# A second bias's column sums in split operands, moved behind a factor product, and one product's banks taken in another order

## The chip, the cores and the metric

The kernel runs on one core of one Trainium2 chip. The metric is the device time of one execution, in microseconds, the median over several runs. TensorE (PE in the views, PEld for its weight loads), VectorE (DVE), ScalarE (ACT), GpSimd (POOL) and SyncE (SP, here a queue that issues transfers) each run their own list of instructions in order and wait for one another through semaphores.

## The reference, cut to what matters

```python
def _L0_cond_ref(x, adapter_mapping, W, b, lora_As, lora_Bs):      # B, T = 8, 256; 1024 in, 1024 out; rank 16
    base_out = jnp.einsum('bti,oi->bto', x, W) + b
    lora_h = jnp.einsum('bti,bir->btr', x, lora_As[adapter_mapping])
    return base_out + jnp.einsum('btr,bro->bto', lora_h, lora_Bs[adapter_mapping]) * 2.0

def _L1_cond_ref(x, adapter_ids, base_weight, base_bias, lora_A_w, lora_B_w):
    result = jnp.einsum('bsd,od->bso', x, base_weight) + base_bias
    h = jnp.einsum('bsd,brd->bsr', x, lora_A_w[adapter_ids])
    return result + jnp.einsum('bsr,bor->bso', h, lora_B_w[adapter_ids])

x = x + _L0_cond_ref(x, itok_B_0_23, W0, b0, A0, B0)
x = x + _L1_cond_ref(x, itok_B_6_15, W1, b1, A1, B1)
```

With U = I + W0 (transposed) and V = I + W1 (transposed) the two layers are one map: x U V, plus a low-rank part for each batch, plus a bias row c = b0 V + b1. The edits concern c.

## The kernel before, in words

**Fused weight (span 0 to about 113 us).** U V, 1024 by 1024, is built from quadrants of 512 by 512 with seven products, M1 to M7, instead of eight. Each operand is split in two float32r numbers, a high part (`high`, a cast on ScalarE) and a low part (`low`, a subtraction on VectorE), and each product of 128x128 weights with a 128x512 operand is three matmuls: high by high, high by low, low by high (L1036, L1040, L1041). A product has four row blocks of twelve matmuls (`row_block`), one to a PSUM bank. `a_banks` are banks 0 to 3, `b_banks` banks 4 to 7.

**Order on TensorE around the change.** M6 adds onto `a_banks`. Then come two matmuls of `ones_b` (128x128 ones in float32) with `bias_sum` (128x1024 float32, the partial products of c, one row to a partition), L1160: they sum over the partitions, into `b_banks[1]` and `b_banks[2]`, and count `c_summed`. Then the factor product `gt_passes` (24 matmuls, L1054 to L1056) goes into `b_banks[0]` and counts `gt_summed`. Then M5, whose row block into a `b_bank` adds onto a copy of M6's `a_bank` that ScalarE puts there (`put_e`, counted by `e_put`), then M4 onto `a_banks`, with a transposition (L1062) after its second block.

**Order on ScalarE there.** `put_e(3)`, the high part of `d11`, the high rows of c (`c_hl[0]`, L551, two copies from the banks), `put_e(1)` and `put_e(2)` (each behind VectorE's low rows of c), `gt_copy(1)` (L429), `put_e(0)`, the high part of `t3`, then the first batch's operands (`high_x`, L462) mixed with the high parts of `d22` (L566) and, later, `d21` (L570).

**Order on VectorE there.** The low parts of b1's rows (L928), `t2` = `d11` + `t3` (L649), the low rows of c (L938), the low part of `d11` (L646), sums of the first batch (L727, L734), the low part of `t3` (L646), the batch's low parts (L720) mixed with those of `d22` (L706, L707), the low part of `t2`, small fills (L964, L968) that end in `pad_set`, then `d21` and `t4` (L713, L715) mixed with `g_copy(1)` (L670) and `factors` (L755 to L759). Place 4 of `ops` holds `us3`, then `us2`, which M6 reads, then `t3`.

**SyncE's queue there.** The rows of b1 (L314) and of c (L322) are written to DRAM, come back as the stacked operand `rb` (L276), and the next batch's x is loaded (L268).

**Batches (from about 113 us).** For each of eight batches TensorE runs `p1` to `p7`, seven products of the fused weight with combinations of x, twelve matmuls each (L1188 to L1190), one product of x with the low-rank factors (`h_product`, L1214), and four matmuls of the stack (`ranks`, L1195). In the first batch the order is p1, p6, h, p7, p2, p5, p4, `fill_z`, p3. Before p1 it waits for `pad_set`; p7 waits for VectorE's `make_u2` (L793), and `fill_z` for `make_u4` (L800). Between these two VectorE runs, in order, the low part of `t1`, `stack_h`, the low part of `t4`, `make_u3` (L806), the second batch's low parts and sums, and the low part of its S2 (L720), whose cast on ScalarE (L462) waits for the sum L734.

Of the kernel before, what the change touches and what calls it, by code (L numbers as in the profile page):

```python
# [5 lines left out]
F32 = mybir.dt.float32  # L6
F32R = mybir.dt.float32r
# [30 lines left out]
def lora_pair(nc, xT, W0, W1T, A0, B0T, A1T, B1, b0, b1, idx0, idx1, out):  # L38
# [15 lines left out]

    ORDER_M7 = (1, 2, 3, 0)
    ORDER_M6 = (2, 3, 0, 1)
    ORDER_LAST = (3, 1, 2, 0)

    with ExitStack() as ctx:
        def sb(name, shape, dt):  # L60
            return ctx.enter_context(nc.sbuf_tensor(name, shape, dt))

        def sem(name):
            return ctx.enter_context(nc.semaphore(name))

        idx = sb("idx", [1, 2 * B], I32)
        ones_b = sb("ones_b", [P, P], F32)
        b0_raw = sb("b0_raw", [P, KT], F32)
        b0_sum = sb("b0_sum", [P, KH], F32)
        ops = sb("ops", [P, 6, 2, QUAD], F32R)  # L70
# [42 lines left out]


        gt_raw = g_all[:, KH:KT, :].rearrange("p k n -> p (k n)")

        def raw(name):
            at = UNIT[name]
# [11 lines left out]
        def d22(part, k):  # L130
            return late[:, 4 + part, k * HALF:(k + 1) * HALF]
# [85 lines left out]
        bias_step = sem("bias_step")  # L217
        st_step = sem("st_step")
        r_summed = sem("r_summed")
        c_summed = sem("c_summed")  # L220
        r_hi = sem("r_hi")
        r_lo = sem("r_lo")
# [128 lines left out]
        @block.gpsimd  # L351
        def _(pool):
            nc.gpsimd.memset(ident[:, :], 0.0).then_inc(ident_made, 1)
            pool.wait_ge(ident_made, 1)
            nc.gpsimd.affine_select(out=ident[:, :], in_=ident[:, :], compare_op=ALU.not_equal, fill=1.0, base=0,
                                    pattern=[[-1, P]], channel_multiplier=1).then_inc(ident_made, 1)
            nc.gpsimd.memset(ones_b[:, :], 1.0)
            nc.gpsimd.memset(same_batch[:, :, :], 1.0).then_inc(masks_made, 1)

            pool.wait_ge(masks_made, 1)  # L360
            nc.gpsimd.affine_select(out=same_batch[:, :, :], in_=same_batch[:, :, :], compare_op=ALU.is_ge, fill=0.0,
                                    base=0, pattern=[[-RK, B], [0, RK]], channel_multiplier=1).then_inc(masks_made, 1)
            pool.wait_ge(masks_made, 2)
            nc.gpsimd.affine_select(out=same_batch[:, :, :], in_=same_batch[:, :, :], compare_op=ALU.is_ge, fill=0.0,
                                    base=RK - 1, pattern=[[RK, B], [0, RK]], channel_multiplier=-1
                                    ).then_inc(masks_made, 1)

            def adapter(b):
                return pool.value_load(idx[0:1, bass.ds(b, 1)], min_val=0, max_val=SLOTS - 1)

            pool.wait_ge(idx_landed, 2 * DMA)
            with pool.Fori(0, B) as b:
                i1 = adapter(b + B)
                pool.dma_start(a1_raw[:, bass.ds(b * BR, BR)],
                               A1T[bass.ds(i1, 1), :, :, :].rearrange("s p k r -> p (s k r)")).then_inc(lora_landed, DMA)
            with pool.Fori(0, B) as b:
                i0 = adapter(b)
                pool.dma_start(b0t_raw[:, bass.ds(b * BR, BR)],
                               B0T[bass.ds(i0, 1), :, :, :].rearrange("s p k r -> p (s k r)")).then_inc(b0t_landed, DMA)

            def load_a0(b):
                i0 = adapter(b)
                if b >= 2:
                    pool.wait_ge(aa_ready, b - 1)
                pool.dma_start(a0_raw[:, b % 2, :], A0[bass.ds(i0, 1), :, :, :].rearrange("s p k r -> p (s k r)")
                               ).then_inc(a0_landed[b % 2], DMA)

            load_a0(0)
            load_a0(1)
            pool.wait_ge(lora_lo, 3)  # L390
            pool.wait_ge(b_sum_made, 1)
            for b in range(B):
                i1 = adapter(B + b)
                pool.dma_start(b1_raw[b * RK:(b + 1) * RK, :],
                               B1[bass.ds(i1, 1), :, :].rearrange("s r n -> (s r) n")).then_inc(b1_landed, DMA)
            for b in range(2, B):
                load_a0(b)

        @block.scalar
        def _(act):  # L400
# [9 lines left out]
            def high(q):  # L410
                nc.scalar.copy(op(q, 0), raw(q)).then_inc(hi[SLOT[q]], 1)  # L411
# [10 lines left out]
            def gt_copy(h):  # L422
                act.wait_ge(gt_summed, h + 1)
                if h == 0:
                    act.wait_ge(lora_lo, 1)
                    act.wait_ge(a_diff_made, 1)
                else:
                    act.wait_ge(g_turned, 1)
                nc.scalar.copy(gt_raw, b_banks[0][:, :]).then_inc(gt_copied, 1)  # L429
# [8 lines left out]
            def put_e(m):  # L438
                act.wait_ge(m_done[6], ORDER_M6.index(m) + 1)
                act.wait_ge(t3_kept, KH)  # L440
                if m == 0:
                    act.wait_ge(gt_copied, 2)
                nc.scalar.copy(b_banks[m][:, :], a_banks[m][:, :]).then_inc(e_put, 1)
# [101 lines left out]
                               ).then_inc(b1_hi_made, 1)  # L545
            put_e(3)
            act.wait_ge(m_done[6], KH)
            high("d11")
            for h in range(NH):
                act.wait_ge(c_summed, h + 1)  # L550
                nc.scalar.copy(c_hl[0][:, h * HALF:(h + 1) * HALF], b_banks[1 + h][0:B, :]).then_inc(c_hi_made, 1)  # L551
            for m in (1, 2):
                act.wait_ge(c_lo_made, m)
                put_e(m)
            gt_copy(1)
            put_e(0)
            high("t3")


# [3 lines left out]

            def high_d22(n):
                act.wait_ge(m_done[5], n + 1)
                nc.scalar.copy(d22(0, ORDER_LAST[n]), b_banks[ORDER_LAST[n]][:, :]).then_inc(hi[SLOT["d22"]], 1)  # L566

            def high_d21(n):
                act.wait_ge(m_done[4], n + 1)
                nc.scalar.copy(op_k("d21", 0, ORDER_LAST[n]), a_banks[ORDER_LAST[n]][:, :]).then_inc(hi[SLOT["d21"]], 1)  # L570

            act.wait_ge(lo[SLOT["vt1"]], filled("vt1", 1))
            act.wait_ge(summed["t2"], 1)
# [42 lines left out]
        def _(dve):  # L616
# [84 lines left out]
                                               ).then_inc(r_lo, 1)  # L701

            def low_d22(n):
                m = ORDER_LAST[n]
                dve.wait_ge(hi[SLOT["d22"]], filled("d22", n + 1))
                nc.vector.tensor_tensor(d22(1, m), b_banks[m][:, :], d22(0, m), ALU.subtract).then_inc(lo[SLOT["d22"]], 1)  # L706
                nc.vector.tensor_tensor(raw_k("t1", m), b_banks[m][:, :], raw_k("t2", m), ALU.subtract  # L707
                                        ).then_inc(summed["t1"], 1)

            def low_d21(n):  # L710
                m = ORDER_LAST[n]
                dve.wait_ge(hi[SLOT["d21"]], filled("d21", n + 1))
                nc.vector.tensor_tensor(op_k("d21", 1, m), a_banks[m][:, :], op_k("d21", 0, m), ALU.subtract  # L713
                                        ).then_inc(lo[SLOT["d21"]], 1)
                nc.vector.tensor_tensor(raw_k("t4", m), a_banks[m][:, :], raw_k("t2", m), ALU.subtract  # L715
                                        ).then_inc(summed["t4"], 1)
# [208 lines left out]
            for h in range(NH):  # L925
                cols = slice(h * HALF, (h + 1) * HALF)
                dve.wait_ge(b1_hi_made, h + 1)
                nc.vector.tensor_tensor(b1_hl[:, 1, cols], b1_raw[:, cols], b1_hl[:, 0, cols], ALU.subtract  # L928
                                        ).then_inc(b1_lo_made, 1)

            dve.wait_ge(t3_kept, KH)
            dve.wait_ge(d11_kept, KH)
# [95 lines left out]
        def _(pe):  # L1028
# [125 lines left out]
                row_block("us2", "vt2", a_banks[m], m, True).then_inc(m_done[6], 1)  # L1154

            pe.wait_ge(t3_kept, KH)
            pe.wait_ge(bias_step, 2 * KT)
            for h in range(NH):
                cols = slice(h * HALF, (h + 1) * HALF)
                mm(b_banks[1 + h][:, :], ones_b[:, :], bias_sum[:, cols], start=True, stop=True).then_inc(c_summed, 1)  # L1160

            pe.wait_ge(lo[SLOT["us1"]], filled("us1", 1))
            pe.wait_ge(lo[SLOT["u22"]], filled("u22", 1))
            pe.wait_ge(a_diff_lo, 1)
            gt_passes("us1", 0, True, False)
            gt_passes("u22", KH, False, True).then_inc(gt_summed, 1)


            pe.wait_ge(lo[SLOT["vt1"]], filled("vt1", 1))
            for n, m in enumerate(ORDER_LAST):  # L1170
                pe.wait_ge(e_put, n + 1)
                row_block("us1", "vt1", b_banks[m], m, True).then_inc(m_done[5], 1)
            pe.wait_ge(lo[SLOT["vt4"]], filled("vt4", 1))
            for n, m in enumerate(ORDER_LAST):
                row_block("u22", "vt4", a_banks[m], m, True).then_inc(m_done[4], 1)
                if n == 1:
                    pe.wait_ge(lo[SLOT["d22"]], filled("d22", 1))
                    pe.wait_ge(summed["t1"], 1)
                    turn(1, b_banks[3])
# [188 lines left out]
```

## Time and profile before

| | |
|---|---|
| median of 3 runs | 293.67 us (293.61 to 294.14) |
| the profiled execution's own time | 294.13 us |
| its span in the trace | 292.30 us |
| TensorE matmul busy | 286.5 us, 98% of the span |
| VectorE busy | 216.1 us, 74% |
| ScalarE busy | 107.1 us, 37% |
| granted TensorE clock | 1.00 of full speed over the span |

The span runs from the first to the last instruction that the profiler saw; the execution's own time has 1.83 us more around it. Busy times overlap, and a matmul's record is longer than its pitch (a record of 0.39 us every 0.23 us), so a busy TensorE need not be at its peak. Idle time of an engine costs only what some other engine then waits for.

### The profile page before, as it was taken

How to read it: one execution, taken by the hardware profiler on the slowest of the kernel's cores; microseconds unless marked ns; L12 is line 12 of the kernel's file. 1: busy time of each engine (PE TensorE's matmuls, PEld its weight loads, DVE VectorE, ACT ScalarE, POOL GpSimd, SP SyncE). 2: the span in 40 equal slices, each digit the busy share in tenths (PEclk: the TensorE clock that was granted, in tenths of full speed). 3: DMA queues.
4: the chain of work that ended last, by engine and by line, in shares of the span. 5: the costliest groups of instructions: out<-in, count | busy, mean ns of one | idle time of the engine just before them, and what ended most of it. 6: DMA issues, size and time to landing. Idle time of an engine off the chain costs nothing.

```text
span 292.3 us, 3869 instructions
## 1 busy us (share of the span) xinstructions
PE 286.5 (98%) x1322; PEld 236.7 (81%) x1322; DVE 216.1 (74%) x331; ACT 107.1 (37%) x150; POOL 18.7 (6%) x43
## 2 busy tenths in 40 slices
PE   7989999999999999999999999999999999999996
PEld 5868788887878888888888888888888888888885
DVE  4778999999798999888774774774774774774313
ACT  4466264244686654433132132132132232231000
POOL 3333201300000001000000000000000000000000
PEclk9999999999999999999999999999999999999999
DMA  7995000100544460003602603603603513512002
GB/s 257 410 411 209 27 1 11 55 9 0 162 166 174 151 188 9 9 36 125 193 36 110 207 36 130 189 36 129 190 37 128 178 38 126 180 38 108 0 36 110
DMA packets 14792, 33.94 MB, mean 116 GB/s; under 512 B 2325, under 2 KB 2581, under 8 KB 14774
## 3 DMA queue, kind: packets, MB, share of 16 engines
q1 hardware_dynamic: 13602, 31.60, 31.1%
q0 software_dynamic: 1024, 2.10, 2.2%
q8 instruction: 11, 0.18, 0.3%
q14 instruction: 7, 0.06, 0.1%
q10 hardware_dynamic: 148, 0.00, 0.0%
HBM read 22.09 MB, written 11.60 MB: 115 GB/s over the span
## 4 chain that ended last, share of the span: by engine, by line
PE 89%; DMA 6%; DVE 1%; SPq 1%; ACT 1%; issue 0%; DVEq 0%
PE bank L1189 17%; PE bank L1188 17%; PE bank L1190 17%; DMA raw_b<-W1T 6%; PE bank L1036 6%; PE bank L1041 6%; PE bank L1040 6%; PE bank L1214 5%; PE bank L1195 3%; PE bank L1054 1%; PE bank L1068 1%; PE bank L1070 1%; PE bank L1069 1%; PE bank L1056 1%; PE bank L1055 1%; DVE raw_b L649 1%
## 5 line engine op out<-in xcount | busy, mean ns | idle before, releaser
L1188 PE MATMUL bank<-ops,late 128*128 128x512 f32 x192 | 74.9, 390 | 0.0
L1189 PE MATMUL bank<-ops,late 128*128 128x512 f32 x192 | 74.9, 390 | 0.0
L1190 PE MATMUL bank<-ops,late 128*128 128x512 f32 x192 | 74.7, 389 | 0.0
L462 ACT CAST late<-raw_a 128x512 fp32r<-128x512 f32 x48 | 29.4, 622 | 63.3 <-PE bank L1195 29.6
L1040 PE MATMUL bank<-ops 128*128 128x512 f32 x112 | 43.6, 390 | 0.0
L1041 PE MATMUL bank<-ops 128*128 128x512 f32 x112 | 43.6, 390 | 0.0
L1190 PEld LDWEIGHTS bank<-ops,late 128*128 128x128 f32 x192 | 36.0, 188 | 7.6
L1189 PEld LDWEIGHTS bank<-ops,late 128*128 128x128 f32 x192 | 36.1, 188 | 7.3
L1188 PEld LDWEIGHTS bank<-ops,late 128*128 128x128 f32 x192 | 36.1, 188 | 7.4
L1036 PE MATMUL bank<-ops 128*128 128x512 f32 x112 | 40.2, 397 | 1.1 <-ACT raw_b L490 1.1
L720 DVE TENSOR_TENSOR late<-raw_a,late 128x512 fp32r<-128x512 f32 x48 | 31.9, 686 | 0.2
L1036 PEld LDWEIGHTS bank<-ops 128*128 128x128 f32 x112 | 20.7, 188 | 6.3 <-issue 1.9
L1040 PEld LDWEIGHTS bank<-ops 128*128 128x128 f32 x112 | 21.0, 188 | 4.7 <-issue 0.4
L1041 PEld LDWEIGHTS bank<-ops 128*128 128x128 f32 x112 | 21.0, 188 | 4.4
L646 DVE TENSOR_TENSOR ops<-raw_a,ops 128x2048 fp32r<-128x2048 f32 x9 | 20.6, 2286 | 1.0 <-ACT ops L411 1.0
L462 ACT CAST late<-rows 128x512 fp32r<-128x512 f32 x16 | 9.8, 623 | 30.3 <-DVE rows L734 26.4
L411 ACT CAST ops<-raw_a 128x2048 fp32r<-128x2048 f32 x9 | 17.1, 1913 | 8.4 <-PE bank L1041 4.3
L765 DVE COPY scratch<-bank 32x256 f32<-32x256 f32 x8 | 3.3, 416 | 21.7 <-PE bank L1214 21.7
L1214 PEld LDWEIGHTS bank<-late,aa 128*128 128x128 f32 x128 | 16.2, 189 | 0.6
L1214 PE MATMUL bank<-late,aa 128*128 128x256 f32 x128 | 16.4, 281 | 0.0
L646 DVE TENSOR_TENSOR ops<-raw_b,ops 128x2048 fp32r<-128x2048 f32 x6 | 13.6, 2286 | 1.9 <-ACT ops L411 1.9
L411 ACT CAST ops<-raw_b 128x2048 fp32r<-128x2048 f32 x6 | 11.5, 1910 | 9.0 <-PE bank L1142 5.2
(149 smaller groups left out, 377.4 us busy)
## 6 DMA issues: line engine op xcount, KB each, us to landing
raw_a<-xT SPq DMA_DIRECT2D x32, 256.0 KB, 4.3
out<-raw_a SPq DMA_DIRECT2D x27, 256.0 KB, 2.0
a<-rb_rows SPq DMA_DIRECT2D x8, 392.0 KB
raw_a<-W1T SPq DMA_DIRECT2D x2, 1024.0 KB, 14.2
raw_b<-W SPq DMA_DIRECT2D x2, 1024.0 KB, 17.5
rb_rows<-late SPq DMA_DIRECT2D x3, 512.0 KB
rb_rows<-b0w SPq DMA_DIRECT2D x3, 512.0 KB
raw_a<-W SPq DMA_DIRECT2D x2, 512.0 KB, 4.8
```

The costliest lines, as they stand in the source:

```text
L411: nc.scalar.copy(op(q, 0), raw(q)).then_inc(hi[SLOT[q]], 1)
L462: nc.scalar.copy(x_op(j, 0), x_raw(j)).then_inc(op_hi[j], 1)
L646: nc.vector.tensor_tensor(op(q, 1), raw(q), op(q, 0), ALU.subtract).then_inc(lo[SLOT[q]], 1)
L720: nc.vector.tensor_tensor(x_op(j, 1), x_raw(j), x_op(j, 0), ALU.subtract).then_inc(op_lo[j], 1)
L1036: return mm(bank[:, :], left(u, 0, k, m), op_k(v, 0, k), start=(k == 0 and not on_top), stop=False, skip_group_check=on_top)
L1040: mm(bank[:, :], left(u, 0, k, m), op_k(v, 1, k), start=False, stop=False, skip_group_check=on_top)
L1041: return mm(bank[:, :], left(u, 1, k, m), op_k(v, 0, k), start=False, stop=(k == KH - 1), skip_group_check=on_top)
L1188: mm(bank[:, :], hi, t_op(t, 0, k), start=(start and k == 0), stop=False, skip_group_check=not start)
L1189: mm(bank[:, :], hi, t_op(t, 1, k), start=False, stop=False, skip_group_check=not start)
L1190: last = mm(bank[:, :], lo, t_op(t, 0, k), start=False, stop=(k == KH - 1), skip_group_check=not start)
L1195: return mm(bank[:, :], h_stack[b % 2][0:STACK, q * P:(q + 1) * P], rb[b % 2][:, h * HALF:(h + 1) * HALF], start=False, stop=True, skip_gr ...
L1214: last = mm(banks[6 + s][:, 0:T], aa[:, s, k * 4 * RK:k * 4 * RK + P], x_first[part][:, 2 * kh:2 * kh + 2, tok], start=(k == 0 and part == ...
```

## The change

The float32 matmuls over `bias_sum` go. Instead ScalarE casts `bias_sum` (128x1024) to a high part behind M6, before the high part of `d11`, and VectorE subtracts to a low part, behind b1's low parts and before `t2`; both lie in place 4 of `ops`, free between M6 and `t3`. TensorE runs four float32r matmuls, two to a bank, behind the factor product instead of ahead of it. `ones_b` becomes float32r. On ScalarE `gt_copy(1)` and `put_e(0)` go ahead of c's high rows. M5, and `d22` that is read from it, take the banks as 3, 0, 1, 2; M4 keeps 3, 1, 2, 0.

```diff
-    ORDER_LAST = (3, 1, 2, 0)
+    ORDER_M5 = (3, 0, 1, 2)
+    ORDER_M4 = (3, 1, 2, 0)
...
-        ones_b = sb("ones_b", [P, P], F32)
+        ones_b = sb("ones_b", [P, P], F32R)
...
+        bias_hl = [ops[:, SLOT["t3"], part, 0:D] for part in range(2)]
...
-            nc.gpsimd.memset(ones_b[:, :], 1.0)
+            nc.gpsimd.memset(ones_b[:, :].bitcast(F32), 1.0)
...
             put_e(3)
             act.wait_ge(m_done[6], KH)
+            act.wait_ge(bias_step, 2 * KT)
+            nc.scalar.copy(bias_hl[0], bias_sum).then_inc(bias_hi, 1)
             high("d11")
+            gt_copy(1)
+            put_e(0)
             for h in range(NH):
                 act.wait_ge(c_summed, h + 1)
                 nc.scalar.copy(c_hl[0][:, h * HALF:(h + 1) * HALF], b_banks[1 + h][0:B, :]).then_inc(c_hi_made, 1)
             for m in (1, 2):
                 act.wait_ge(c_lo_made, m)
                 put_e(m)
-            gt_copy(1)
-            put_e(0)
             high("t3")
...
                                         ).then_inc(b1_lo_made, 1)
+            dve.wait_ge(bias_hi, 1)
+            nc.vector.tensor_tensor(bias_hl[1], bias_sum, bias_hl[0], ALU.subtract).then_inc(bias_lo, 1)
...
             pe.wait_ge(t3_kept, KH)
-            pe.wait_ge(bias_step, 2 * KT)
-            for h in range(NH):
-                cols = slice(h * HALF, (h + 1) * HALF)
-                mm(b_banks[1 + h][:, :], ones_b[:, :], bias_sum[:, cols], start=True, stop=True).then_inc(c_summed, 1)
-
             pe.wait_ge(lo[SLOT["us1"]], filled("us1", 1))
             pe.wait_ge(lo[SLOT["u22"]], filled("u22", 1))
             pe.wait_ge(a_diff_lo, 1)
             gt_passes("us1", 0, True, False)
             gt_passes("u22", KH, False, True).then_inc(gt_summed, 1)
 
+            pe.wait_ge(bias_lo, 1)
+            for h in range(NH):
+                cols = slice(h * HALF, (h + 1) * HALF)
+                mm(b_banks[1 + h][:, :], ones_b[:, :], bias_hl[0][:, cols], start=True, stop=False)
+                mm(b_banks[1 + h][:, :], ones_b[:, :], bias_hl[1][:, cols], start=False, stop=True
+                   ).then_inc(c_summed, 1)
+
 
             pe.wait_ge(lo[SLOT["vt1"]], filled("vt1", 1))
-            for n, m in enumerate(ORDER_LAST):
+            for n, m in enumerate(ORDER_M5):
                 pe.wait_ge(e_put, n + 1)
                 row_block("us1", "vt1", b_banks[m], m, True).then_inc(m_done[5], 1)
             pe.wait_ge(lo[SLOT["vt4"]], filled("vt4", 1))
-            for n, m in enumerate(ORDER_LAST):
+            for n, m in enumerate(ORDER_M4):
                 row_block("u22", "vt4", a_banks[m], m, True).then_inc(m_done[4], 1)
```

The helpers `high_d22` and `low_d22` take their banks from `ORDER_M5`, `high_d21` and `low_d21` theirs from `ORDER_M4`.

## Rows read from the trace of the kernel before

**Rows 1.** The page: busy time, then the chain that ended last by engine.

```profile
PE 286.5 (98%) x1322; PEld 236.7 (81%) x1322; DVE 216.1 (74%) x331; ACT 107.1 (37%) x150; POOL 18.7 (6%) x43
...
PE 89%; DMA 6%; DVE 1%; SPq 1%; ACT 1%; issue 0%; DVEq 0%
```

**Rows 2.** The waits of PEld, 84 to 292 us: in total, times, longest.

```profile
PEld bank L1195 <- DVE raw_a L800: 0.3, 1, 0.3
```

**Rows 3.** The chain that ended last, 72 to 108 us: start, duration, what.

```profile
84.05 1.72 PE bank L1160 x4
85.76 0.23 PE bank L1054
...
91.25 0.23 PE bank L1036
```

**Rows 4.** Groups of instructions by shape, 0 to 60 us, ACT and DVE.

```profile
L408 ACT CAST ops<-raw_a 128x1024 fp32r<-128x1024 f32 x4 | 4.0, 1049 | 2.7 <-DMA raw_a<-W1T 1.7 <-DMA raw_a<-W 1.1
...
L641 DVE TENSOR_TENSOR ops<-raw_a,ops 128x1024 fp32r<-128x1024 f32 x4 | 4.7, 1222 | 2.5 <-ACT ops L408 2.5
```

**Rows 5.** The timeline of ACT from 84 us: start, duration, instruction, idle before.

```profile
84.08 1.91 ACT L411 CAST ops<-raw_b 128x2048 fp32r<-128x2048 f32 x1 [0.30 <-PE bank L1041]
85.89 1.05 ACT L551 CAST c_rows<-bank 8x512 fp32r<-8x512 f32 x2
89.14 1.17 ACT L443 COPY bank<-bank 128x512 f32<-128x512 f32 x2 [2.20 <-DVE c_rows L938]
91.28 0.59 ACT L429 COPY g_all<-bank 128x512 f32<-128x512 f32 x1 [0.98 <-PE bank L1056]
91.98 0.57 ACT L443 COPY bank<-bank 128x512 f32<-128x512 f32 x1
92.46 1.92 ACT L411 CAST ops<-raw_a 128x2048 fp32r<-128x2048 f32 x1
```

**Rows 6.** The timeline of DVE from 84 us.

```profile
86.11 2.28 DVE L649 TENSOR_TENSOR raw_a<-raw_b,raw_a 128x2048 f32<-128x2048 f32 x1
88.42 1.28 DVE L938 TENSOR_TENSOR c_rows<-bank,c_rows 8x512 fp32r<-8x512 f32 x2
89.73 2.29 DVE L646 TENSOR_TENSOR ops<-raw_b,ops 128x2048 fp32r<-128x2048 f32 x1
91.94 0.68 DVE L727 TENSOR_TENSOR rows<-raw_a 128x512 f32<-128x512 f32 x1
92.73 0.69 DVE L734 TENSOR_TENSOR rows<-rows,raw_a 128x512 f32<-128x512 f32 x1
94.41 2.29 DVE L646 TENSOR_TENSOR ops<-raw_a,ops 128x2048 fp32r<-128x2048 f32 x1 [0.99 <-ACT ops L411]
...
110.44 0.19 DVE L968 MEMSET aa<- 128x64 f32 x2
...
117.07 0.68 DVE L715 TENSOR_TENSOR raw_a<-bank,raw_a 128x512 f32<-128x512 f32 x1
118.98 0.69 DVE L793 TENSOR_TENSOR raw_a<-bank,rows 128x512 f32<-128x512 f32 x1 [1.22 <-PE bank L1190]
...
130.75 0.69 DVE L720 TENSOR_TENSOR late<-rows,late 128x512 fp32r<-128x512 f32 x1 [0.69 <-ACT late L462]
131.36 0.69 DVE L800 TENSOR_TENSOR raw_a<-bank,raw_a 128x512 f32<-128x512 f32 x1
```

**Rows 7.** The timeline of PEld: where p1, p7 and `fill_z` of the first batch start.

```profile
113.11 0.19 PEld L1188 LDWEIGHTS bank<-ops,late 128*128 128x128 f32 x1
...
120.55 0.19 PEld L1188 LDWEIGHTS bank<-ops,late 128*128 128x128 f32 x1
...
132.10 0.19 PEld L1195 LDWEIGHTS bank<-a,b0w 98*128 98x128 f32 x1 [0.31 <-DVE raw_a L800]
```

**Rows 8.** The timeline of SP's queue: start, duration, what it issues.

```profile
90.49 3.32 SPq L322 DMA_DIRECT2D rb_rows<-c_rows  x2
99.47 0.74 SPq L276 DMA_DIRECT2D a<-rb_rows  x2
```

More of the change, by code:

```diff
@@ L219, in lora_pair @@
         r_summed = sem("r_summed")
+        bias_hi = sem("bias_hi")
+        bias_lo = sem("bias_lo")
         c_summed = sem("c_summed")
@@ L565, in high_d22 @@
                 act.wait_ge(m_done[5], n + 1)
-                nc.scalar.copy(d22(0, ORDER_LAST[n]), b_banks[ORDER_LAST[n]][:, :]).then_inc(hi[SLOT["d22"]], 1)
+                nc.scalar.copy(d22(0, ORDER_M5[n]), b_banks[ORDER_M5[n]][:, :]).then_inc(hi[SLOT["d22"]], 1)
             def high_d21(n):
                 act.wait_ge(m_done[4], n + 1)
-                nc.scalar.copy(op_k("d21", 0, ORDER_LAST[n]), a_banks[ORDER_LAST[n]][:, :]).then_inc(hi[SLOT["d21"]], 1)
+                nc.scalar.copy(op_k("d21", 0, ORDER_M4[n]), a_banks[ORDER_M4[n]][:, :]).then_inc(hi[SLOT["d21"]], 1)
             act.wait_ge(lo[SLOT["vt1"]], filled("vt1", 1))
@@ L703, in low_d22 @@
             def low_d22(n):
-                m = ORDER_LAST[n]
+                m = ORDER_M5[n]
                 dve.wait_ge(hi[SLOT["d22"]], filled("d22", n + 1))
@@ L710, in low_d21 @@
             def low_d21(n):
-                m = ORDER_LAST[n]
+                m = ORDER_M4[n]
                 dve.wait_ge(hi[SLOT["d21"]], filled("d21", n + 1))
```

## The prediction

> **What bounds the kernel now.** I read the page first. TensorE is busy for 98% of the span and holds 89% of the chain that ended last [rows 1], so almost every microsecond on TensorE counts. The exceptions are its waits, and from 84 us on only one of them is for another engine: the weight load of `fill_z` in the first batch waited 0.3 us for L800, which is `make_u4` on VectorE [rows 2]. That small wait matters more than the 98%: it says that at 132 us TensorE and VectorE arrive together, TensorE a little early. A saving on TensorE ahead of that point is lost there unless VectorE comes earlier too, and a delay of VectorE is passed on to the end in full. Next I read the chain around the change for prices on TensorE [rows 3], then the orders of ScalarE and VectorE from there to `make_u4` [rows 5, 6], to see how far a shift in them travels, and last the starts of the three products that wait for VectorE [rows 7].
>
> **TensorE's own saving.** The two float32 matmuls appear as four pieces, 1.72 us of the chain, from 84.05, when M6 ends, to 85.76 [rows 3]. The 24 matmuls of the factor product behind them take 91.25 - 85.76 = 5.49 us, 0.229 each; each streams 512 columns, as the four new ones will. New: 4 x 0.229 = 0.92. The saving is 1.71 - 0.92 = 0.79 us. If the float32r pitch did not hold for weights of ones, the nearest row is the old price of a piece, 0.43 us: no saving then, and M5 starts as before. So 0 to 0.79; I take 0.79, because the operands have the same type and shape as the factor product's. The Trainium skill, "TensorE: Matmul & The Clock Gate", section "Back-to-back issue gap", puts an isolated warm gap at N / 2.4 + 2.5 ns, 216 ns for 512 columns. The trace disagrees by 13 ns a matmul; by the page the saving would be 0.85 instead of 0.79.
>
> The factor product now runs from 84.05 to 89.54, the new sums to 90.46, and M5 begins there, not at 91.25.
>
> **The split of the bias row.** A 128x1024 cast on ScalarE takes 1.05 us, a 128x1024 subtraction on VectorE 1.22 [rows 4]. The cast starts where `d11` started, 84.08 [rows 5], and is done by 85.1. VectorE is free for it at 86.11, where `t2` starts now [rows 6], so the low part is done by 87.3. TensorE asks for it at 89.54: hidden, with 2.2 us to spare. `d11` on ScalarE ends near 87.0, in a gap that lasts until 89.14 [rows 5]. The cover on TensorE is the factor product; without it the cast and subtraction would cost some 3 us.
>
> On VectorE nothing hides it. Its queue moves on by the pitch of such an instruction, about 1.14 (the record less the 0.08 that neighbours overlap), so `t2` runs from 87.25 to 89.53.
>
> **The rows of c come later: the term that decides.** Now c's high rows stand on ScalarE behind `gt_copy(1)` and `put_e(0)`. Step by step [rows 5]: `gt_copy(1)` starts 0.03 after the factor product, 89.57. `put_e(0)` starts 0.70 after it (91.98 - 91.28): 90.27. The next copy starts 0.48 after that (92.46 - 91.98): 90.75. It takes 0.57 (the pair takes 1.05 with that pitch): 91.31. The sums themselves are in the banks by 90.0 and 90.46, so it is ScalarE's order that counts. VectorE starts c's low rows at 91.34. Before, it found the high rows ready and went straight from `t2` to them, at 88.42 [rows 6]. So c's low rows start 91.34 - 88.42 = 2.92 us later. Of that 1.14 is the new subtraction and 1.8 is a new wait, in which VectorE's whole list stands behind the waiting instruction: `d11`'s low part, the sums S1 and S2, `t3`'s low part, the batch's low parts, `d22`, `t2`, the fills, `d21`.
>
> How much of the 2.92 survives? The next idle time of VectorE is before `t3`'s low part, which now waits until 94.41 for ScalarE's cast. Its new time: 91.34 + 1.31 (c's low rows) + 2.21 (`d11`) + 0.79 (S1) + 0.60 (S2) = 96.25, the steps from the starts in [rows 6] and 0.60 for the pitch of a 128x512 pair. ScalarE has `put_e(1)` and `put_e(2)` done and starts `t3`'s cast near 93.14, ends at 95.05, so it no longer holds VectorE. The lag is 96.25 - 94.41 = 1.84 us. From there to 117.07 VectorE's timeline has no wait (the stretch between the two rows in [rows 6]), so all of it arrives there 1.84 late.
>
> The bounds of this lag: if VectorE never waited for c's high rows, 1.14 less the old idle time of about 1.0, some 0.1 us; if each of the five hand-overs cost 0.1 more than the rows give, 2.34. I take 1.84, since each step has a row of its own.
>
> **Where the lag meets TensorE, by rows 7.** p1 could start its weight load at 113.11 - 0.79 = 112.32. `pad_set` comes from L968, 110.44 + 0.19 + 1.84 = 112.47 [rows 6]: a wait of 0.2 us, new. `make_u2` (L793): VectorE sat idle 1.22 before it, waiting for p6. With the 0.08 of overlap it could have started at 117.67. Late by 1.84 it starts at 119.51, no longer held by p6. It started at 118.98, so it is 0.53 later, and ends at 120.20. p7 could have started at 120.55 - 0.79 = 119.76; it starts at 120.25, still 0.30 ahead of before, after a wait of about 0.3 (the 0.2 at p1 comes out of the same saving). From `make_u2` to `make_u4` VectorE has only one idle time, 0.69 for ScalarE's cast of S2 [rows 6], and that cast waits for VectorE's own sum, so it moves along. `make_u4` ends at 132.05 + 0.53, and `fill_z` starts at 132.10 + 0.53 = 132.63, after a wait that grows from 0.3 to about 1.1.
>
> Behind it TensorE runs without a wait on another engine to the end [rows 2], and VectorE is late by no more than TensorE is. So the whole is + 0.53 us: the 0.79 is all waited away, and 0.53 besides. In general the change costs (lag - 1.31) when that is above -0.79.
>
> **What costs nothing.** The bank order: M5's first block is on bank 3 (put before), its second on bank 0, put by 90.84 and wanted at 90.46 + 2.74 = 93.2; `put_e(1)` is ready near 92.7 and wanted at 95.9. If `put_e` were late by more than 3 us it would hold M5. M4's transposition uses bank 3, still first. SyncE: c's rows go out from 92.65, not 90.49, so the stack's loads move from 99.47 to about 101.7 [rows 8], and are first wanted at p2, 126 us. The fill L964 waits for the same write and starts at 111.7. The ones have the same size as before.
>
> **The rivals.**
> A, TensorE keeps its saving: 293.67 - 0.79 = 292.88. For it: TensorE's share of the chain [rows 1]. It is also the Trainium skill's rule, "Perfetto Trace Analysis", section "Identifying the Most-Contended Engine": the one with the highest occupancy is to be optimized first. The trace speaks against applying it here, by the row of the 0.3 us wait. Needed: a lag of at most 0.52 us, that is VectorE hardly waiting for c's rows. 9%.
> B, nothing: the saving and a lag near 1.31 cancel, 293.7. It needs c's rows 0.5 us earlier than summed. 6%.
> C, clearly slower. The place is ScalarE's run `gt_copy(1)`, `put_e(0)`, c's first row, and the hand-over to VectorE. If ScalarE cannot start c's row 0.48 behind `put_e(0)` but waits for its completion, and the same at the next hand-over, each costs 0.1 to 0.2, and all of it reaches `fill_z`. It decides from 0.06 us above my sum. With 0.3 more: 293.67 + 0.83 = 294.50. For it: `put_e(0)` itself starts 0.11 after the end of `gt_copy` [rows 5]. Against: `t3`'s cast started before `put_e(0)` had ended. 41%.
> D, no effect at all (float32r sums as slow as float32) would leave the lag and give 294.2 to 295; its 1% is in C.
>
> **How the numbers follow.** The profiled execution takes 294.13 us around a span of 292.30; with + 0.53 the span would be 292.83 and that execution 294.66. The median of the runs is 293.67, so the forecast is 293.67 + 0.53 = 294.20. What a measurement of this kernel can tell from no change is about 0.2%, 0.59 us; the forecast lies just inside. It has 44% by itself (294.0 to 294.26). Faster is A, 9%. Within 0.2%: the forecast and B, 50%. Slower is C, 41%. The range is 293.5 to 294.8: it takes in B, the forecast and C up to a lag 0.6 above my sum, and leaves out A and the rest of C.
>
> **What would show it.** Right: the four sums in 0.92 us behind the factor product, near 90 us; VectorE idle for about 1.8 us before c's low rows with ScalarE's copy as releaser; no idle time before `t3`'s low part; waits of TensorE at p1, p7 and `fill_z` of about 0.2, 0.3 and 1.1 us; `fill_z` starting near 132.6. Wrong: VectorE idle before `make_u2` again (lag under 1.3), or TensorE waiting for `bias_lo` or for `put_e` in M5, or a new wait in a later batch.

## The result, and the profile after

The changed kernel takes 294.38 us (median of 19 runs, 293.54 to 295.18), the kernel before, timed with it, 293.54 (19 runs, 292.48 to 294.14). The ratio is 1.0031, with a 95% interval of 1.0021 to 1.0041: slower, by 0.9 us (the medians differ by 0.84).

The profiled execution of the changed kernel has the shorter span, 291.8 us against 292.3. That is no contradiction. M6 ends at 82.77 us in it, not at 84.05, because the first loads of the weights happened to land sooner: the chain that ended last has them as one piece. Here it is for the changed kernel, start and duration in us: the transfer, the first matmul behind M6, and the last matmul.

```profile
5.02 17.50 DMA raw_b<-W1T
...
82.77 0.23 PE bank L1064
...
288.84 0.13 PE bank L1261
```

The same piece took 18.85 us in the kernel before, from 4.90 to 23.75, whose last matmul stands in its chain so:

```profile
289.37 0.13 PE bank L1249
```

From the landing of this transfer to the end of M6 both kernels take the same: 84.05 - 23.75 = 60.30 us before, 82.77 - 22.52 = 60.25 after. So I count from the end of M6 to the end of the last matmul. Before: 289.50 - 84.05 = 205.45 us [rows 3]. After: 288.97 - 82.77 = 206.20. The part of the kernel that the change touches got 0.75 us longer. Two profiles of the same kernel agree in this number to 0.02 us, where the measured times of one kernel spread over 1.6 us; it carries most of what follows.

Not all of the loss lies there. The execution's own time has more around the span than before. Over all runs, time less span is 1.95 us on average for the changed kernel (19 runs), and 1.78, 1.78 and 1.75 for the kernel before in the three later timings (33, 32 and 29 runs), with a standard deviation of 0.05 to 0.08 from run to run. That is 0.19 us more outside the span; with the 0.75 it makes 0.94, where 0.84 to 0.91 was measured.

The waits of the changed kernel's PEld, 80 to 292 us (total, times, longest), where before the only wait for another engine was one of 0.3 [rows 2]:

```profile
PEld bank L1207 <- DVE raw_a L808: 1.1, 1, 1.1
PEld bank L1200 <- issue: 0.5, 1, 0.5
PEld bank L1200 <- DVE aa L978: 0.2, 1, 0.2
```

L1207 waiting for L808 is `fill_z` waiting for `make_u4`. L1200 is a weight load of p1 (released by the fill L978, that is `pad_set`) and of p7. For the second the view names nobody; the load starts at 119.18, and `make_u2` (L801) has ended at 119.11. The same three in the timeline of PEld, which answers to [rows 7]; `fill_z` starts 48.77 us after the end of M6 instead of 48.05, 0.72 late:

```profile
111.22 0.19 PEld L1200 LDWEIGHTS bank<-ops,late 128*128 128x128 f32 x1 [0.24 <-DVE aa L978]
...
119.18 0.19 PEld L1200 LDWEIGHTS bank<-ops,late 128*128 128x128 f32 x1 [0.53 <-issue]
...
131.54 0.19 PEld L1207 LDWEIGHTS bank<-a,b0w 98*128 98x128 f32 x1 [1.11 <-DVE raw_a L808]
```

The timeline of the changed kernel's ScalarE, which answers to [rows 5]:

```profile
82.81 1.05 ACT L555 CAST ops<-rows 128x1024 fp32r<-128x1024 f32 x1 [0.27 <-PE bank L1051]
83.77 1.91 ACT L417 CAST ops<-raw_b 128x2048 fp32r<-128x2048 f32 x1
88.25 0.59 ACT L435 COPY g_all<-bank 128x512 f32<-128x512 f32 x1 [2.57 <-PE bank L1066]
88.94 0.57 ACT L449 COPY bank<-bank 128x512 f32<-128x512 f32 x1
89.43 1.05 ACT L561 CAST c_rows<-bank 8x512 fp32r<-8x512 f32 x2
```

And of its VectorE, which answers to [rows 6]:

```profile
84.87 1.22 DVE L939 TENSOR_TENSOR ops<-rows,ops 128x1024 fp32r<-128x1024 f32 x1
86.00 2.29 DVE L657 TENSOR_TENSOR raw_a<-raw_b,raw_a 128x2048 f32<-128x2048 f32 x1
90.03 1.28 DVE L948 TENSOR_TENSOR c_rows<-bank,c_rows 8x512 fp32r<-8x512 f32 x2 [1.74 <-ACT c_rows L561]
91.34 2.29 DVE L654 TENSOR_TENSOR ops<-raw_b,ops 128x2048 fp32r<-128x2048 f32 x1
...
94.95 2.29 DVE L654 TENSOR_TENSOR ops<-raw_a,ops 128x2048 fp32r<-128x2048 f32 x1
...
117.61 0.68 DVE L723 TENSOR_TENSOR raw_a<-bank,raw_a 128x512 f32<-128x512 f32 x1
118.42 0.69 DVE L801 TENSOR_TENSOR raw_a<-bank,rows 128x512 f32<-128x512 f32 x1
```

Take 82.77 from each start, and 84.05 from those of before. Then c's low rows start at 7.26 instead of 4.37, with a new idle time of 1.74 us ahead of them. The low part of `t3` starts at 12.18 instead of 10.36, and its old idle time of 0.99 is gone. The last `t4` (L723) starts 1.82 late, at 34.84. `make_u2` starts at 35.65 instead of 34.93, 0.72 late, and is no longer held by TensorE.

### The profile page after: what moved, and what is told of

Same layout as the page of the kernel before. It is cut to its first block, busy times and chain, and to the rows that moved or that the text cites. A ratio compares the mean times of both kernels' runs of the same rounds, so it can differ in the third digit from the quotient of the medians.

```text
span 291.8 us, 3872 instructions
## 1 busy us (share of the span) xinstructions
PE 285.8 (98%) x1322; PEld 236.7 (81%) x1322; DVE 217.1 (74%) x332; ACT 107.8 (37%) x151; POOL 18.6 (6%) x43
## 4 chain that ended last, share of the span: by engine, by line
PE 74%; DVE 12%; DMA 6%; ACT 3%; issue 2%; SPq 1%; DVEq 0%; ACTq 0%
PE bank L1201 15%; PE bank L1200 15%; PE bank L1202 15%; DMA raw_b<-W1T 6%; PE bank L1226 5%; PE bank L1046 4%; PE bank L1051 4%; PE bank L1050 4%; PE bank L1207 2%; DVE ops L654 2%; DVE late L728 2%; PE bank L1064 1%; PE bank L1078 1%; PE bank L1080 1%; PE bank L1079 1%
## 5 line engine op out<-in xcount | busy, mean ns | idle before, releaser
L1200 PE MATMUL bank<-ops,late 128*128 128x512 f32 x192 | 75.1, 391 | 0.4 <-issue 0.4
L1200 PEld LDWEIGHTS bank<-ops,late 128*128 128x128 f32 x192 | 36.1, 188 | 8.1 <-issue 0.5
```

Of the source, the lines that this page charges most:

```text
L1200: mm(bank[:, :], hi, t_op(t, 0, k), start=(start and k == 0), stop=False, skip_group_check=not start)
```

## The experiments

All times in this table are counted from the end of M6, from the timelines of each profile. "Last t4" is the last VectorE instruction before `make_u2`; its lag is against the kernel before. The last column is measured time against the kernel before, with the 95% interval of the ratio; 0.1% is 0.29 us. "Changed" is the changed kernel, and rows without "before" in their name are versions of it.

| kernel | c's low rows | last t4 (lag) | make_u2 | to the last matmul | measured |
|---|---|---|---|---|---|
| before | 4.37 | 33.02 | 34.93 | 205.45 | |
| changed | 7.26 | 34.83 (1.81) | 35.64 | 206.20 | +0.31% (0.21 to 0.41) |
| changed, once more | 7.26 | 34.83 (1.81) | 35.64 | 206.19 | +0.43% (0.25 to 0.60) |
| old order on ScalarE | 6.54 | 34.13 (1.11) | 34.94 | 205.46 | +0.17% (0.04 to 0.29) |
| no split, moved only | 7.26 | 34.82 (1.80) | 35.63 | 206.15 | +0.28% (0.11 to 0.45) |
| d11 first on VectorE | 7.70 | 34.10 (1.08) | 34.92 | 205.47 | -0.08% (-0.33 to 0.17) |
| make_u4 earlier | 7.25 | 34.83 (1.81) | 35.65 | 205.25 | -0.01% (-0.15 to 0.13) |
| before, four fills | 4.39 | 35.12 (2.10) | 35.94 | 206.47 | +0.46% (0.32 to 0.60) |
| before, two fills | 4.40 | 34.05 (1.03) | 34.93 | 205.45 | -0.04% (-0.20 to 0.11) |
| before, half the sums | 4.38 | 32.17 (-0.85) | 34.07 | 204.60 | -0.31% (-0.46 to -0.16) |
| three moves | 7.76 | 33.13 (0.11) | 34.10 | 204.63 | -0.12% (-0.23 to 0.00) |
| three moves, once more | 7.70 | 33.08 (0.06) | 34.11 | 204.64 | -0.16% (-0.40 to 0.07) |
| three moves and make_u4 earlier | 7.70 | 33.06 (0.04) | 34.10 | 204.50 | -0.30% (-0.53 to -0.06) |

**The changed kernel once more.**

> The changed kernel once more, beside the others. By its profile, VectorE reaches t3's low part 1.82 us late counted from the end of M6, the idle time before make_u2 absorbs 1.10 of it, and fill_z starts 0.72 us late. Expected: 0.7 to 0.9 us slower than the kernel before.

From M6 to the last matmul it is the same to 0.01 us. The measured loss, 0.43% or 1.3 us, is larger than the 0.7 to 0.9 expected; with the 0.19 outside the span, 0.94 us (0.32%) would be right, and that is inside its interval.

**One part undone: the order on ScalarE and the banks of M5.**

```diff
-            gt_copy(1)
-            put_e(0)
             for h in range(NH):
                 act.wait_ge(c_summed, h + 1)
...
                 put_e(m)
+            gt_copy(1)
+            put_e(0)
             high("t3")
```

with `ORDER_M5 = (3, 1, 2, 0)`.

> The changed kernel with one part undone: ScalarE takes c's high rows, put_e(1), put_e(2), gt_copy(1), put_e(0) in the old order, and M5 the banks 3, 1, 2, 0. Theory H (VectorE's wait for c's high rows, made by ScalarE's new order, is what makes it slower): c's high rows start when the first sum is in its bank, 5.98 us after the end of M6 instead of 6.66, c's low rows at 6.60 instead of 7.26; t3's cast then holds VectorE until 11.54, so the lag is 1.2 instead of 1.8, and the whole takes 0.1 us more than the kernel before, 0.65 less than the changed one. Rival S (the new subtraction's own 1.1 us on VectorE makes it slower, wherever c's rows stand): no change against the changed kernel, 0.7 to 0.9 slower than before. Rival B (the bank order matters by itself): M5 shows a wait on TensorE.

Theory H held. The wait of VectorE for c's high rows shrinks from 1.74 to 1.04 us. From this kernel's VectorE timeline (M6 ends at 83.92):

```profile
90.46 1.28 DVE L948 TENSOR_TENSOR c_rows<-bank,c_rows 8x512 fp32r<-8x512 f32 x2 [1.04 <-ACT c_rows L559]
```

The lag becomes 1.11, `make_u2` starts where it did before the change, and 0.74 us are won back. The subtraction is still there, so rival S falls. M5 shows no wait in either order. The measured time is a miss: 0.50 us above the kernel before (0.12 to 0.85), where 0.1 was expected. Of this 0.19 lies outside the span (1.97 us over its 12 runs). Against the changed kernel in the same timing it is 0.26% less, 0.76 us, which agrees with the 0.74.

**The move alone, without the split.**

```diff
-                mm(b_banks[1 + h][:, :], ones_b[:, :], bias_hl[0][:, cols], start=True, stop=False)
-                mm(b_banks[1 + h][:, :], ones_b[:, :], bias_hl[1][:, cols], start=False, stop=True
-                   ).then_inc(c_summed, 1)
+                mm(b_banks[1 + h][:, :], ones_b[:, :], bias_sum[:, cols], start=True, stop=True).then_inc(c_summed, 1)
```

with the cast, the subtraction and the new type of `ones_b` taken out again.

> The changed kernel without the split: the two float32 sums stay float32 and only move behind the factor product; no cast and no subtraction of the bias row. Theory H: c's low rows still start 7.26 us after the end of M6, because ScalarE's order sets them, so VectorE's wait before them grows from 1.7 to 2.9 us and the lag stays 1.8; TensorE's 0.79 us are not saved, but they were waited away anyway. So 0.7 to 0.9 us slower than before, the same as the changed kernel. Rival S (the subtraction's time on VectorE): lag 0.7, and 0 to 0.1 us slower than before.

```profile
84.95 2.29 DVE L655 TENSOR_TENSOR raw_a<-raw_b,raw_a 128x2048 f32<-128x2048 f32 x1
90.13 1.28 DVE L944 TENSOR_TENSOR c_rows<-bank,c_rows 8x512 fp32r<-8x512 f32 x2 [2.88 <-ACT c_rows L559]
```

Without the subtraction `t2` is done 1.1 us sooner, and VectorE waits 1.1 longer, 2.88 us. The lag is the same. In the changed kernel the split therefore costs VectorE nothing and brings TensorE nothing that reaches the end: from M6 on, the move accounts for 0.70 of the 0.75 us. Outside the span it is another matter: this kernel has 1.74 us there, as little as the kernel before.

**VectorE's order alone.** The changed kernel with `low("d11")` ahead of c's low rows.

> The changed kernel with only d11's low part ahead of c's low rows on VectorE. It fills the wait of 1.7 us; c's low rows start 7.7 us after the end of M6 instead of 7.26. put_e(1) and put_e(2) and so t3's cast come 0.4 later, the cast ends near 11.5, and t3's low part starts there: a lag of 1.1 to 1.2, 0.0 to 0.1 us slower than before from M6 to the last matmul, 0.65 less than the changed kernel.

```profile
91.91 1.28 DVE L949 TENSOR_TENSOR c_rows<-bank,c_rows 8x512 fp32r<-8x512 f32 x2
...
95.65 2.29 DVE L654 TENSOR_TENSOR ops<-raw_a,ops 128x2048 fp32r<-128x2048 f32 x1 [0.94 <-ACT ops L417]
```

The wait before c's rows is gone, and 0.94 us of it come back before `t3`'s low part: `put_e(1)` and `put_e(2)` wait for c's low rows, and `t3`'s cast stands behind them on ScalarE. The lag is 1.08 and the loss is gone.

**The dose.** The kernel before with idle fills on VectorE behind the first batch's low parts, four or two of them:

```diff
+            dve.wait_ge(lo[SLOT["t3"]], filled("t3", 1))
+            for k in range(4):
+                nc.vector.memset(raw_k("t4", k), 0.0)
             dve.wait_ge(lo[SLOT["vt4"]], filled("vt4", 1))
```

> The kernel before with four fills of 128x512 on VectorE behind the first batch's low parts, into space that is dead there: nothing else is changed. They delay VectorE by about 1.7 us. By the rule read from the changed kernel's trace (of a lag of VectorE 1.10 us is absorbed before make_u2, the rest reaches fill_z): 0.6 us slower than before. Rival: VectorE's lateness is not what costs, and the time stays as before.

> The same with two fills: a delay of about 0.85 us, below 1.10. By the rule it is absorbed whole before make_u2: 0.0 us from the end of M6 to the last matmul, and the measured time that of the kernel before. Rival (any lag is paid in proportion): 0.3 us slower.

The fills took 0.51 to 0.53 us each instead of the 0.42 assumed, so the lags are 2.10 and 1.03. The rule gives 2.10 - 1.10 = 1.00 and 0; from M6 to the last matmul they are 1.02 and 0.00. Both rivals fall: the lag does cost, and not in proportion. The idle time before `make_u2` shows it. Two fills, then four:

```profile
117.69 0.68 DVE L715 TENSOR_TENSOR raw_a<-bank,raw_a 128x512 f32<-128x512 f32 x1
118.57 0.69 DVE L793 TENSOR_TENSOR raw_a<-bank,rows 128x512 f32<-128x512 f32 x1 [0.20 <-PE bank L1193]
```

```profile
119.64 0.68 DVE L715 TENSOR_TENSOR raw_a<-bank,raw_a 128x512 f32<-128x512 f32 x1
120.46 0.69 DVE L793 TENSOR_TENSOR raw_a<-bank,rows 128x512 f32<-128x512 f32 x1
```

With two it is still p6 that releases `make_u2`. With four `make_u2` follows the last `t4` at a distance of 0.82.

**Where the lateness is passed on.**

```diff
             sum_s2(1)
+            make_u4(0)
             low_x(S2, 1)
-            make_u4(0)
```

> The changed kernel with one move: in the first batch VectorE runs make_u4 before the low part of S2 instead of behind it, in the 0.69 us in which it now waits for ScalarE's cast of S2. Theory H says that all of the loss is passed on at one place, fill_z waiting for make_u4: with make_u4 about 1.3 us earlier fill_z does not wait, p7 starts 0.1 us ahead of the kernel before, and from the end of M6 to the last matmul the time is 0.2 us shorter than before, 0.9 to 1.0 shorter than in the changed kernel. Rival T (VectorE's lateness is passed on elsewhere too, in later batches): a new wait of TensorE behind fill_z, and less than 0.5 us won back.

`make_u4` starts 0.61 us behind the sum L742, and the two weight loads at `fill_z` stand together in one row, with no idle time between them:

```profile
130.24 0.69 DVE L742 TENSOR_TENSOR rows<-rows,raw_a 128x512 f32<-128x512 f32 x1
130.85 0.68 DVE L808 TENSOR_TENSOR raw_a<-bank,raw_a 128x512 f32<-128x512 f32 x1
```

```profile
131.67 0.42 PEld L1207 LDWEIGHTS bank<-a,b0w 98*128 98x128 f32 x2
```

VectorE is as late as in the changed kernel up to `make_u2`, and yet 0.95 us are won back. So `fill_z` is where the loss of the change reached the end; rival T falls. Only 0.20 us of TensorE's 0.79 are kept, for its waits at p1 and p7 are still there (0.24 and 0.57). The measured time, 0.01% below before, does not tell 205.25 from 205.45.

**Is a saving on TensorE worth anything there?** The kernel before with only the first of the two sums. The upper half of c is then not computed, so the result is wrong and only the time counts; ScalarE's second copy no longer waits for a sum of its own.

> The kernel before with the second float32 sum left out (the upper half of the bias row c is then not computed). TensorE has 0.86 us less ahead of the factor product and VectorE's list is as before, so VectorE can follow: make_u2 is held by p6 today with 1.10 us to spare. By theory H the saving is kept whole, 0.8 to 0.9 us faster than before. Rival W (a saving on TensorE ahead of fill_z is always waited away, since make_u4 is late already): as before.

0.86 us fewer on TensorE, 0.85 fewer to the last matmul, 0.31% measured. All of VectorE's stations move along: counted from the end of M6, c's low rows start at 4.38 as before, and the last `t4` and `make_u2` come 0.85 us earlier. Rival W falls: a saving on TensorE is worth something there as long as VectorE keeps pace.

**A version that does.** Three moves in the changed kernel: on ScalarE c's high rows first and `t3`'s cast before `put_e(1)`, on VectorE `d11` first.

```diff
-            gt_copy(1)
-            put_e(0)
             for h in range(NH):
                 act.wait_ge(c_summed, h + 1)
...
+            gt_copy(1)
+            put_e(0)
+            high("t3")
             for m in (1, 2):
                 act.wait_ge(c_lo_made, m)
                 put_e(m)
-            high("t3")
...
+            low("d11")
             for h in range(NH):
...
-            low("d11")
```

> The changed kernel with three moves: ScalarE takes c's high rows before gt_copy(1) and put_e(0), and t3's cast before put_e(1) and put_e(2); VectorE takes d11's low part before c's low rows. Theory H: d11's low part fills VectorE's wait, c's low rows start 7.7 us after the end of M6 with nothing idle, t3's cast ends at 10.0 and its low part starts at 10.4, as before the change (10.36): a lag of 0.0 to 0.1. Then make_u4 no longer holds fill_z, TensorE keeps its 0.79 us, and the whole is 0.7 to 0.8 us faster than before. Rival P (the float32r sums with ones, or their place, cost TensorE something that the chain does not show): not faster than before. Rival S: the subtraction's 1.1 us remains, 0 to 0.1 us slower than before.

> The version with three moves once more, beside the two others: 204.63 us from the end of M6 to the last matmul, 0.82 less than before. In the first timing it was 0.35 us faster than before; if the missing 0.5 is the spread of the first transfers, it will be between 0.4 and 1.0 faster here.

> The earlier version with c's high rows first, t3's cast before put_e(1), d11's low part before c's low rows, and now make_u4 before the low part of S2. That version's fill_z still waited 0.3 us for make_u4; this wait goes. From the end of M6 to the last matmul: 0.15 us shorter than that version (204.63), 1.0 shorter than the kernel before (205.45). Measured: 0.5 to 1.0 us faster than before.

VectorE's list has no idle time of note between `t2` and `t3`'s low part. Of the version with three moves:

```profile
85.78 2.28 DVE L657 TENSOR_TENSOR raw_a<-raw_b,raw_a 128x2048 f32<-128x2048 f32 x1
87.98 2.29 DVE L654 TENSOR_TENSOR ops<-raw_b,ops 128x2048 fp32r<-128x2048 f32 x1
90.30 1.28 DVE L949 TENSOR_TENSOR c_rows<-bank,c_rows 8x512 fp32r<-8x512 f32 x2
...
93.01 2.29 DVE L654 TENSOR_TENSOR ops<-raw_a,ops 128x2048 fp32r<-128x2048 f32 x1
```

From M6 on it keeps TensorE's saving: 0.82 us less than before, and 0.95 with `make_u4` moved as well, after which no wait of PEld is left behind M6. So rivals P and S fall for this stretch. The measured times say 0.12, 0.16 and 0.30% faster; only the last interval keeps clear of no change, and the expected 0.7 to 0.8 us of the first was not met by its measured 0.35. The other two, 0.47 and 0.88 us, lie inside what was expected of them.

**What the time outside the span adds.** Averaged over all runs of each kernel, it falls into three groups:

| kernels | outside the span, us |
|---|---|
| changed, and its five versions with the split (eight timings) | 1.94 to 1.98 |
| before, before with half the sums, no split | 1.74 to 1.78 |
| before with two or four fills | 1.60, 1.61 |

So about 0.2 us comes with the split. With it, the versions with three moves should be 0.6 to 0.8 us faster than before, and not 0.8 to 0.95. What takes this time no view shows. It lies ahead of the first instruction or behind the last, and the fills, with 0.17 less, show that other edits move it too. Sums of both parts lie inside the interval for every timed kernel but the one with four fills (0.85 us summed, interval 0.94 to 1.76). What is left between sum and measurement, 0.5 us at most either way, is within the spread of the first loads. Ahead of M6 nothing else differs: in 11 of the 13 profiles the chain goes back to the landing of `raw_b`, and the end of M6 is 60.25 to 60.30 us behind it in all of them.

## Why the prediction was right or wrong

**The direction and the place were right.** The forecast was + 0.53 us from TensorE's waits, the runs show + 0.75 from M6 on and 0.8 to 0.9 measured; 294.38 lies in the range. That it is only 0.18 above 294.20 is in part luck: two terms of 0.2 us each were missing from the sum, and the kernel before, timed again, came out 0.13 below the 293.67 that the forecast stood on. The likeliest case, "within 0.2%", was not what came: the ratio of 1.0031 lies above it, in the case called clearly slower. C's size came true, but not at C's place. C put a price of the hand-over at ScalarE's run and the step to VectorE, and it was paid at `make_u2`; ScalarE's run `gt_copy(1)`, `put_e(0)`, c's first row took 0.69 and 0.49, as summed (0.70 and 0.48).

**TensorE's own saving** held. The four sums have the pitch of the matmuls around them, 0.23 us, in the changed kernel's TensorE timeline:

```profile
88.05 0.39 PE L1176 MATMUL bank<-ops,ones_b 128*128 128x512 f32 x1
88.28 0.39 PE L1177 MATMUL bank<-ops,ones_b 128*128 128x512 f32 x1
88.51 0.39 PE L1176 MATMUL bank<-ops,ones_b 128*128 128x512 f32 x1
88.74 0.40 PE L1177 MATMUL bank<-ops,ones_b 128*128 128x512 f32 x1
88.97 0.39 PE L1046 MATMUL bank<-ops 128*128 128x512 f32 x1
```

The split was hidden from TensorE, which never waited for `bias_lo`.

**The rows of c and the lag** held: 7.26 from the end of M6 where 7.29 was summed, a wait of 1.74 where 1.8 was, a lag of 1.81 where 1.84 was.

**What the next idle time absorbs: the term that was mis-sized.** "With the 0.08 of overlap it could have started at 117.67", and so "the change costs (lag - 1.31)". The right figure is 1.10. `make_u2` in the first batch waits for all four `t4`, which VectorE itself makes, the last one directly before it. Here an instruction that waits for the result of its neighbour loses the overlap and pays for the hand-over: it starts 0.81 us behind the last `t4` (118.42 - 117.61), where the pitch is 0.60. While p6 released `make_u2` this distance was hidden, and no row of the kernel before shows it there. That is 0.21 us, nearly all of what the forecast missed from M6 on. The rows point to the neighbour's result as what costs, and not to the number of waits; no run changes this one wait alone. In the second batch's sums of the changed kernel, L735 waits for three semaphores, none of them its neighbour's, and starts 0.60 behind the instruction before it (three of them take 1.80 from start to start); L742 waits for L735's sum and starts 0.82 behind it:

```profile
126.19 1.89 DVE L728 TENSOR_TENSOR late<-raw_a,late 128x512 fp32r<-128x512 f32 x3
127.99 0.69 DVE L735 TENSOR_TENSOR rows<-raw_a 128x512 f32<-128x512 f32 x1
128.81 0.69 DVE L742 TENSOR_TENSOR rows<-rows,raw_a 128x512 f32<-128x512 f32 x1
```

The price was on record before: the same pair, L727 and L734, is 0.79 apart in [rows 6], and the forecast used this 0.79 as the step from S1 to S2 but not again at `make_u2`. ScalarE's rows show it too: `put_e(0)` follows `gt_copy(1)`, for whose end it waits, at 0.70, and is itself followed at 0.48 [rows 5]. The Trainium skill, "ScalarE: Activation LUTs", section "What ACT_TABLE_LOAD costs", says that back-to-back ACTIVATEs overlap by about 93 ns; the trace agrees for the free neighbour (0.57 - 0.48 = 0.09), and the dependent one gets none of it.

**The three waits** were forecast at about 0.2, 0.3 and 1.1 us; they are 0.24, 0.53 and 1.11. The middle one carries the 0.2 again.

**The time outside the span: a term that was not in the sum.** The forecast put the same time around the span after the change as before it. It is 0.19 us more, and it comes with the split. Why stays open.

**The rivals.** A (the saving is kept) was wrong for this kernel, and right as soon as VectorE is not late, which three experiments show. B's condition, a lag near the absorbed time, is what the old order on ScalarE gives, and it costs 0.01 us from M6 on. The bank order cost nothing, as said: M5 shows no wait in either order, and the versions with three moves keep the new one. No wait of TensorE names a transfer. The stack's loads start 16.23 us after the end of M6 instead of 15.42, 0.8 later and not the 2.2 of the forecast.

## What to carry to other kernels

An engine that is busy for 98% of the span can still be paced by another one at a single place, and a wait of 0.3 us in the profile is enough to show it. Before work is shifted to the other engine or its inputs are made later, follow that engine's list from the edit to that place, add up what arrives late, and subtract each idle time on the way, counted from the earliest start that the code allows. Where an instruction waits for its own neighbour's result, that earliest start is later than the usual pitch, here by 0.2 us. And when the start of a kernel scatters by more than the change can bring, count from an event behind the scatter, but compare the time outside the span as well: here it held 0.19 us of the loss.

## What the runs showed of the hardware that was not expected

The first loads vary from run to run: the chain's piece from the issue to the landing of the last weights needed took 17.50 us in one profile and 18.99 in another, with nothing changed in them. The end of M6 lay between 82.5 and 84.5 us in the profiles, while the 205 us behind it repeated to 0.02. In two profiles, both of the version with three moves, the chain does not go back to a load but through TensorE's own matmuls; M6 ended at 82.5 and 82.9 in them, among the earliest.

The time outside the span differs from kernel to kernel, from 1.60 to 1.98 us, with a standard deviation of at most 0.08 for each.

A fill of 128x512 in a stretch of VectorE without idle time took 0.51 to 0.53 us (1.02 for two in a row, 2.11 for four).
